# Two-part fp16 attention features with stacked heads, and neighbour counts from an extra mask column, in a four-layer graph kernel

## What is computed

```python
# layer 0: graph attention, 4 heads of 16
feats   = einsum('bnf,hfo->bhno', x, kernel)
f_self  = einsum('bnf,hfd->hbnd', x, attention_kernel)
f_other = einsum('bnf,hfd->hbdn', x, attention_kernel_2)
s = adj * einsum('hbnd,hbdm->hbnm', f_self, f_other)
s = where(s >= 0, s, 0.2 * s) / 4 + where(adj == 0, -1e9, 0)
attn = softmax(s, -1) * (adj != 0)
x = layernorm(x + relu(einsum('bhnm,bhmo->bhno', attn, feats) + bias))
# layer 1: A = adj + eye
x = layernorm(x + (A @ x) / sum(A, -1))
# layer 2
x = layernorm(x + adj @ (x @ weight) + bias2)
# layer 3
t = adj @ x
x = layernorm(x + where(t > 0.5, 1, 0))
```

## Time and profile before

| | us |
|---|---|
| median of 3 runs | 1572.43 |
| the 3 runs | 1569.07, 1574.97, 1572.43 |
| span of the profiled execution, first to last instruction | 1570.0 |
| median less that span | 2.4 |
| PE busy in the profile | 1379.7 (88%) |
| DVE busy | 1273.9 (81%) |
| ACT busy | 1235.0 (79%) |
| POOL busy | 1061.9 (68%) |

### The profile page before, as it was taken

One profiled execution on the slowest core, in us unless ns is written; L12 is line 12 of the kernel. 1 busy time (PEld: TensorE's weight loads), 2 busy tenths in 40 slices (PEclk: granted clock), 3 DMA queues, 4 the chain that ended last, 5 costly groups with the idle time before them and its releaser, 6 DMA issues.

```text
span 1570.0 us, 21762 instructions
## 1 busy us (share of the span) xinstructions
PE 1379.7 (88%) x7584; PEld 689.3 (44%) x7584; DVE 1273.9 (81%) x1518; ACT 1235.0 (79%) x1428; POOL 1061.9 (68%) x566
## 2 busy tenths in 40 slices
PE   4698799999899999999989988999899989799766
PEld 2343344454445444444444544454444444345323
DVE  1689789888898878888878888988889878878864
ACT  2598788887888878888878888888888888788631
POOL 3176866778677766787657876777767876776412
PEclk9899789999999989999979999999999999999977
DMA  7634433343433433343433434335333433200000
GB/s 107 111 42 81 47 73 67 56 54 58 88 43 77 47 65 62 58 71 38 83 62 54 57 52 95 45 64 61 51 75 62 69 38 73 58 14 16 26 11 10
DMA packets 144980, 91.16 MB, mean 58 GB/s; under 512 B 102420, under 2 KB 132570, under 8 KB 144858
## 3 DMA queue, kind: packets, MB, share of 16 engines
q1 hardware_dynamic: 129382, 70.44, 21.0%
q0 software_dynamic: 14288, 18.70, 14.8%
q10 hardware_dynamic: 1200, 0.63, 0.2%
HBM read 103.33 MB, written 21.38 MB: 79 GB/s over the span
## 4 chain that ended last, share of the span: by engine, by line
PE 50%; DVE 15%; issue 13%; ACT 9%; POOL 9%; DMA 2%; SPq 1%; ACTq 0%; DVEq 0%; POOLq 0%
PE M L607 10%; PE Z L568 10%; PE M L662 9%; PE Z L570 8%; POOL LS L501 7%; DVE RP L904 5%; ACT LS L754 5%; PE Z L581 4%; DVE LS L918 4%; PE Z L676 3%; PE Z L616 2%; ACT LS L762 2%; DMA adj_cast<-in_adj_dram 1%; PE Z L730 1%; DVE X L1000 1%
## 5 line engine op out<-in xcount | busy, mean ns | idle before, releaser
L501 POOL TENSOR_TENSOR LS<-LS,MB 125x1000 f32<-125x1000 f32 x372 | 871.1, 2359 | 360.7 <-DVE LS L918 264.8
L754 ACT ACTIVATE LS<-Z 125x1000 f32<-125x1000 f32 x576 | 576.3, 1002 | 143.5 <-PE Z L570 142.6
L762 ACT ACTIVATE LS<-LS 125x1000 f32<-125x1000 f32 x576 | 596.7, 1037 | 70.5 <-POOL LS L501 53.8
L904 DVE TENSOR_TENSOR RP<-LS,RP 125x1000 f32<-125x1000 f32 x480 | 575.4, 1199 | 88.3 <-ACT LS L754 66.3
L568 PE MATMUL Z<-AT,BI 126*125 126x500 fp8e4 x1152 | 375.9, 409 | 104.7 <-ACT LS L754 73.9
L570 PE MATMUL Z<-FS,FO 96*125 96x500 bf16 x1152 | 353.1, 388 | 0.0
L607 PE MATMUL M<-LS,V 125*18 125x500 f32 x2304 | 318.3, 626 | 5.5 <-ACT LS L762 5.5
L918 DVE TENSOR_TENSOR LS<-LS,MB 125x1000 f32<-125x1000 f32 x204 | 306.1, 1505 | 7.7 <-DMA MB<-row_maxima 2.4
L568 PEld LDWEIGHTS Z<-AT,BI 126*125 126x125 bf16 x1152 | 126.7, 142 | 418.2 <-ACT LS L754 219.2
L570 PEld LDWEIGHTS Z<-FS,FO 96*125 96x125 bf16 x1152 | 164.5, 143 | 95.0 <-issue 14.8
L662 PE MATMUL M<-AT,XP 125*128 125x500 fp8e4 x756 | 192.3, 377 | 0.0
(11 more groups left out here) (136 smaller groups left out, 885.0 us busy)
## 6 DMA issues: line engine op xcount, KB each, us to landing
MB<-row_maxima SPq DMA_DIRECT2D x48, 500.0 KB, 4.0
adj_cast<-in_adj_dram POOLq DMA_DIRECT2D x96, 183.1 KB, 4.4
FO<-PARTS SPq DMA_DIRECT2D x180, 46.9 KB, 2.1
FS<-PARTS SPq DMA_DIRECT2D x180, 46.9 KB, 2.1
XP<-in_x_dram SPq DMA_DIRECT2D x8, 336.0 KB
XA<-in_x_dram SPq DMA_DIRECT2D x8, 336.0 KB
out_dram<-X SPq DMA_DIRECT2D x7, 375.0 KB
AT<-adj_cast SPq DMA_TRANSPOSE x144, 2.8
```

Of the source, the lines that this page charges most:

```text
L501: nc.gpsimd.tensor_tensor(rows, rows, MB[:P, u % 2, :, :], ALU.subtract).then_inc(sub_pool, 1)
L754: nc.scalar.activation(LS[:P, q % RL, :, :], banks("Z", q)[:P], ACT.Prelu, alpha=SLOPE).then_inc(bent, 1)
L762: nc.scalar.activation(rows, rows, ACT.Exp, scale=0.25).then_inc(exps, 1)
L904: nc.vector.tensor_tensor(run, rows, run, ALU.max).then_inc(maxed, 1)
```

## The change

1. **Two fp16 parts.** `TERMS` has four pairs of two parts instead of six pairs of three. ACT's `middle` and DVE's `rest` are gone; `low` takes the difference straight from PSUM to the second part. `SPARE`, `MIDDLES`, `LOWS` and two semaphores are gone.
2. **Heads stacked.** `FS` holds the 2 x 64 rows of a pair of heads. `FO` keeps one plane for each head, with zeros in the 64 rows of the other, so a score matmul runs over 128 rows instead of 96. `FO` is set to zero once, at the start.
3. **Neighbour counts.** `BI` gets a 126th column of ones, so the mask matmul writes the sums of a tile's columns to row 125 of `Z`. ACT bends 126 rows, and `V` gets a 126th row that is one in the 18th column of the even heads and zero elsewhere. `weigh` contracts over 126 rows and so collects the counts. `degrees` and `DS` are gone, and `weigh` starts its sums in every unit.
4. **Rows in an own buffer.** `XF` no longer shares memory; its load waits for "XT" of the graph before, and `square` no longer waits for "XT".
5. `LS` has 26 slots instead of 24. `GROUP` = 1 and `CUTS` = 3 write the old order in another way.

```diff
+PD = P + 1
-TERMS = [(0, 0), (0, 1), (0, 2), (1, 0), (1, 1), (2, 0)]
+TERMS = [(0, 0), (0, 1), (1, 0), (1, 1)]
...
-RL = 24
+RL = 26
...
-MIDDLES = {19: 0, 26: 1, 31: 2}
-LOWS = {18: 0, 27: 1, 32: 2}
...
-        FS = sb("FS", [KS, H, N], bf16)
-        FO = sb("FO", [KS, H, N], bf16)
+        FS = sb("FS", [2 * KS, PAIRS, N], f16)
+        FO = sb("FO", [2 * KS, H, N], f16)
-        V = sb("V", [P, 2, NT, H, VC], f32)
+        V = sb("V", [PD, 2, NT, H, VC], f32)
-        PARTS = sb("PARTS", [128, 3, N], bf16)
+        PARTS = sb("PARTS", [128, 2, N], f16)
-        XF = SQ
+        XF = sb("XF", [P, NT, F], f32)
-        BI = sb("BI", [P + 1, P], bf16)
+        BI = sb("BI", [PD, PD], bf16)
...
             def load_parts(dst, sem_, side, h):
                 for n, pair in enumerate(TERMS):
-                    sp.dma_start(dst[n * D:(n + 1) * D],
+                    first = h % 2 * KS + n * D
+                    sp.dma_start(dst[first:first + D],
                                  PARTS[side * F + h * D:side * F + (h + 1) * D, pair[side], :]).then_inc(sem_, 16)
...
                 load_parts(FO[:, h, :], fo_in[p], 1, h)
-                load_parts(FS[:, h, :], fs_in[p], 0, h)
+                load_parts(FS[:, p, :], fs_in[p], 0, h)
...
-                        sp.wait_ge(dve_seq, link_of(b - 2, 3, 2))
+                    if b:
+                        sp.wait_ge(m1_filled, counted["XT", b, NS - 1] + 1)
+                    else:
+                        sp.wait_ge(pre_x, NS)
                     load_rows(b + 1, XF, xf_in)
...
-                    nc.tensor.matmul(z[:P, hh, :], BI[:, :], AT[:P + 1, g % RS, pair, PAD:CP, k], start=True, stop=False)
+                    nc.tensor.matmul(z[:PD, hh, :], BI[:, :], AT[:P + 1, g % RS, pair, PAD:CP, k], start=True, stop=False)
...
                     last = nc.tensor.matmul(z[:P, hh, :], FO[:, 2 * p + hh, m * P:(m + 1) * P],
-                                            FS[:, 2 * p + hh, s * C:(s + 1) * C], start=False, stop=True)
+                                            FS[:, p, s * C:(s + 1) * C], start=False, stop=True)
...
-            def degrees(u):
...
-                    last = nc.tensor.matmul(M0[VW * n:VW * n + VC, 0:C], V[:, b % 2, e % STEPS, 2 * p + hh, :], LS[:P, e % RL, hh, :],
-                                            start=(p == 1 and j == 0), stop=(j == STEPS // 2 - 1), skip_group_check=True)
+                    last = nc.tensor.matmul(M0[VW * n:VW * n + VC, 0:C], V[:, b % 2, e % STEPS, 2 * p + hh, :], LS[:PD, e % RL, hh, :],
+                                            start=(j == 0), stop=(j == STEPS // 2 - 1), skip_group_check=True)
...
-                nc.scalar.activation(LS[:P, q % RL, :, :], banks("Z", q)[:P], ACT.Prelu, alpha=SLOPE).then_inc(bent, 1)
+                nc.scalar.activation(LS[:PD, q % RL, :, :], banks("Z", q)[:PD], ACT.Prelu, alpha=SLOPE).then_inc(bent, 1)
...
-                nc.scalar.activation(PARTS[:, 1, c * C:(c + 1) * C], rest, ACT.Copy).then_inc(mid_ready, 1)
...
-                if l == 0 and b + 2 < B:
-
-                    act.wait_ge(m1_filled, counted["XT", b + 2, NS - 1] + 1)
                 nc.scalar.activation(SQ, Y[:, :, :], ACT.Square).then_inc(squared, 1)
...
+            nc.vector.memset(FO[:, :, :].rearrange("k h n -> k (h n)").bitcast(f32), 0.0)
+            nc.vector.memset(V[96:PD, :, :, :, 0:D + 1], 0.0).then_inc(v_set, 1)
+            nc.vector.memset(V[:, :, :, 0:H:2, D + 1:D + 2], 1.0).then_inc(v_set, 1)
+            nc.vector.memset(V[:, :, :, 1:H:2, D + 1:D + 2], 0.0).then_inc(v_set, 1)
...
-            def rest(b, c, bank, rest_):
...
-                nc.vector.tensor_tensor(PARTS[:, 2, c * C:(c + 1) * C], rest_, PARTS[:, 1, c * C:(c + 1) * C],
+                nc.vector.tensor_tensor(PARTS[:, 1, c * C:(c + 1) * C], bank[:, 0:C], PARTS[:, 0, c * C:(c + 1) * C],
                                         ALU.subtract).then_inc(lo_ready, 1)
```

More of the change, by code:

```diff
@@ L35 @@
 TURN = 3
+GROUP = 1
 LAG = 18
@@ L261, in y_at @@
         def y_at(q):
-            for n in range(3 * NS):
+            for n in range(CUTS * NS):
                 at = layer_at(q, Y0 + n)
                 if at and at[1] < 3:
-                    return (*at, *divmod(n, 3))
+                    return (*at, *divmod(n, CUTS))
             return None
@@ L286, in adj_resnorm @@
         for q in range(END):
-            if q < QN:
-                ring.append(("Z", q))
+            if q < QN and q % GROUP == 0:
+                for n in range(GROUP):
+                    ring.append(("Z", q + n))
             if w_at(q):
@@ L549, in ring_free, with masks @@
                     pe.wait_ge(added, 9 * b + 3 * l + c + 1)
-            def fill_z(q):
+            def masks(q):
                 u, m = divmod(q, STEPS)
@@ L582, in turn_run @@
                 last.then_inc(run_turned, 1)
-            def degrees(u):
-                b, i = divmod(u, UPG)
-                g = NS * b + i
-                pe.wait_ge(o4_ready, u + 1)
-                for n in range(NS):
-                    for k in range(ST):
-                        nc.tensor.matmul(M0[VW * k:VW * k + VC, 0:C], DS[:, :], AT[:P, g % RS, KK * n + k // KK, PAD:CP, k % KK],
-                                         start=(n == 0), stop=False, skip_group_check=True)
             def weigh(w):
@@ L660, in collect @@
                     pe.wait_ge(xp_ready, 3 * b + l + 1)
-                for m in range(ST * part, ST * (part + 1)):
+                for m in range(NT // CUTS * part, NT // CUTS * (part + 1)):
                     last = nc.tensor.matmul(M1[:, 0:C], XP[:, m, :], AT[:P, (NS * b + c) % RS, m // KK, PAD:CP, m % KK],
                                             start=(m == 0), stop=(m == NT - 1 and l > 0))
-                if part == 2 and l == 0:
+                if part == CUTS - 1 and l == 0:
                     last = own_rows(M1, c)
-                if part == 2:
+                if part == CUTS - 1:
                     last.then_inc(m1_filled, 1)
@@ L701, in _ @@
             for q in range(END):
-                if q < QN:
-                    fill_z(q)
+                if q < QN and q % GROUP == 0:
+                    for n in range(GROUP):
+                        masks(q + n)
+                    for n in range(GROUP):
+                        scores(q + n)
                 if feature_at(q):
@@ L707, in _ @@
                     collect(*y_at(q))
-                if unit_at(q, DEGREE_AT) is not None and unit_at(q, DEGREE_AT) % UPG < NS:
-                    degrees(unit_at(q, DEGREE_AT))
                 if w_at(q):
@@ L835, in _ @@
                 for n, pair in enumerate(TERMS):
-                    act.dma_start(FS[n * D:(n + 1) * D, h, :], PARTS[h * D:(h + 1) * D, pair[0], :]).then_inc(fs_in[0], 16)
+                    first = h * KS + n * D
+                    act.dma_start(FS[first:first + D, 0, :], PARTS[h * D:(h + 1) * D, pair[0], :]).then_inc(fs_in[0], 16)
             act.wait_ge(ones_in, 1)
@@ L849, in _ @@
                     square(*layer_at(q, SQUARE))
-                if r in MIDDLES and b + 1 < B:
-                    middle(b + 1, MIDDLES[r], REST[:, :])
-                if q < QN:
-                    bend(q)
+                if q < QN and q % GROUP == 0:
+                    for n in range(GROUP):
+                        bend(q + n)
                 at = layer_at(q, HIGH)
```

61 lines of the change are left out of this document (27 added, 34 removed).

## The result

The changed kernel takes 1550.29 us (median of 4 runs, 1540.79 to 1557.14), against 1573.7 for the kernel before on the same chip: a ratio of 0.9863, with a 95% interval of 0.9816 to 0.9909. The recorded ratios come from the single runs and are not exactly the quotient of the two medians, which is 0.985 here. A second set on another chip (e11) gave 0.9881 (0.9851 to 0.9910); a seventh execution of that set took 2461.22 us, 1.6 times as long as the six others, and is left out of it. So the change makes the kernel faster by 1.2 to 1.4%, some 19 to 23 us, where I had forecast 39.5 us. The profiled execution is the slowest of the four: 1557.14 us, a span of 1555.3 and a mean granted clock of 0.931. The four clocks were 0.931, 0.940, 0.939 and 0.945 for 1557.14, 1546.63, 1553.94 and 1540.79 us.

A forecast was written before the change was run, and what follows sets the result against it. No engine was full: ACT set a floor of 1.81 us a step, with further ACT work, PE-bound stretches and stalls above. Terms 14.4 + 5.2 + 6.0 + 7.1 + 1.4 + 5.4 = 39.5 us gave 1533 us, range 1512 to 1560.

The forecast's parts named there:

- rival A: After r=20, PE becomes the new wait at r=23; 18.4 us less gain, 1551 us; chance 0.20.
- the queue's: Sign of right: row_maxima issued within 0.3 us of the reduction's end, MB 2.2 us later, no ACT idling at r=20.
- B: Rival: PE loses up to 17.8 us of work, new slow-clock stretches cost 5.45 us each, say 1609 us; chance 0.17.
- Fewer DMAs of parts: SP's queue: 8 instead of 12 DMAs per head remove ACT's stalls at r=20 in graphs 2 to 7; 14.4 us.
- D: Rival: the store still blocks the maxima in SP's queue; 5.5 us less gain, 1538 us; chance 0.55 together with the forecast.
- Graph 0: ACT's waits at r=17 and 20 go, 5.2 us; its wait for maxima behind r=39 and 41 goes, 6.0 us.
- Fewer parts to make: ACT loses its middle copies; those at r=19 and 31 in seven graphs win 0.51 us each, 7.1 us.
- My bound of 0: Lower bound of the 7.1 us for ACT's removed copies, if PE or POOL is next.
- The clock of graph 4: The half-speed stretch at r=22 to 27 after the 2.25 us stall goes; 5.4 us, bounds 0 and twice that.
- Start, own buffer, score matmul: Kernel-start memsets, separate row buffer and 128-row fp16 score matmuls: no gain or cost; uncovered memsets would cost 4.5 us once.
- The counts: Removing PE's bursts of 12 matmuls wins 0.2 us at r=35 in seven graphs, 1.4 us; upper bound 17.8 us.

The follow-up runs named there:

- e11: The changed kernel itself, unaltered, run again on another chip, against the kernel before: ratio 0.9881.
- e3: The changed kernel with four further DMAs per head into a tile nothing reads (12 again) and 24 slots of LS: 1580.17 us, ratio 1.0051.
- e7: The changed kernel with POOL's low part of the layer input one step later (LOW 6 instead of 5): 1545.46 us, ratio 0.9887.
- e4: The changed kernel with POOL's four adjacency loads moved from r=27, 29, 31, 33 to r=36, 38, 40, 42: 1551.40 us, ratio 0.9863.
- e2: The kernel before without its bursts of 12 matmuls, neighbour counts left out: 1578.35 us, ratio 1.0033.
- e9: The changed kernel with bursts of 12 matmuls that nothing reads, at r=35, 47 and 11: 1520.96 us, ratio 0.9709.
- e1: The changed kernel with bursts of 12 matmuls that nothing reads put back at r=23, 35 and 47: 1538.21 us, ratio 0.9770.
- e12: e1 unaltered, run again on another chip, against the kernel before: 1537.48 us, ratio 0.9808.

## Why the prediction was partly right

The measured 1550 us lies in the range of 1512 to 1560, and 17 us above the forecast of 1533. It lies next to the 1551 of rival A, but A's main step, a new wait at r = 23 to 26, did not happen. The range reached so far up because of A; that it also covered the loss of clock at r = 35 and 47 is in part luck. Of the signs that I had named, the queue's came true as right, and the clock of 0.931 with long steps in new places came true as wrong (B).

- **Fewer DMAs of parts (14.4 us): right, mechanism and size.** ACT's stalls at r = 20 of graphs 2 to 7 are gone, and these steps are 13.9 us shorter; the maxima left 0.03 us after they were ready, and `MB` followed in 2.08 us (2.2 forecast). e3 shows that the DMA count does this. Rivals A and D fall: no wait appears at r = 23 to 26, and the store is out of the way at 768.12.
- **Graph 0 (5.2 and 6.0 us).** The second came as 6.5. The first came as 3.9 (r = 16, 17 and 20): `row_maxima` was issued at 64.52 and `MB` only at 68.43, 3.9 us later and not 2.2, so ACT still waits 1.42 and 0.81 us for POOL.
- **Fewer parts to make (7.1 us): half.** r = 18 and r = 30 are 0.5 us shorter in seven graphs each, and r = 26 gave nothing on balance, as said. But what r = 30 gave, r = 33 took back with interest. The failed step is "in stretches where ACT sets the pace": it did at r = 31, but not two steps on: summed over r = 30 to 33, graphs 1 to 6 are 0.1 to 0.4 us longer than before. Next was POOL, whose low part waits for ACT's high part (shown by e7, after e4 had ruled out the loads) and whose subtraction behind it takes 0.4 us more than before. My bound of 0 for "PE or POOL is next" was the right one for this half.
- **The clock of graph 4 (5.4 us): right.** 19.22 us became 13.78. This was no chance of one execution: in e2, which keeps the old queue, the same steps of graph 4 take 18.71 us at a clock of 0.58, and in e3, where the stalls are back, graphs 2 to 6 take 15.2 to 16.3 us at 0.73 to 0.78.
- **Start, own buffer, score matmul (0): no cost shows.** The first `bend` starts at 36.75 us, before at 36.77. A pair of score matmuls takes 0.59 us at full clock in both kernels, with 96 rows of bf16 and with 128 of fp16. e9 takes r = 46 to 50 in the same 7.98 us as the kernel before.
- **The counts (1.4 us): wrong, in sign and size.** The failed step is "Below nothing the term cannot go by the burst itself", with the clock left out of the term. The row at r = 47 was read rightly: the burst lay in PE's wait and its own time was worth nothing. What I did not ask is what PE does in that wait once the burst is gone. At r = 47 it idles 1.33 us instead of 0.59, and the clock falls in all eight graphs; at r = 35 it idles 1.41 to 1.62 us instead of 0.67 at most, and the clock falls in five. That cost 21.2 us at these two places in the profiled execution, which was the slowest of the four, and 11 to 12 us in the medians (e1, e12). Even the 0.2 us at r = 35 were not the burst's: r = 34 to 38 take 9.74 us in graph 4 both with it (e1) and without.
- **Rival B** had this mechanism ("PE loses up to 17.8 us of work") with a wrong price. I took 5.45 us for a new slow stretch, from one six-step stretch in graph 4. The new ones cost 0.8 to 2.5 us each, and hold for 2 to 4 steps. I also set B against my forecast, one or the other. In truth both happened at once: with the bursts put back the change wins 30 to 34 us (1567.94 - 1537.48 in e12, 1572.04 - 1538.21 in e1), and B takes a third of that.

In the sum: against 39.5 us forecast stand 30 to 34 us with the clock loss taken out. The 6 to 9 us between are the copy at r = 31, the 1.3 us in graph 0 and the counts, and what is left is within the spread of the executions. The 11 to 12 us that are missing beyond that are the clock. Four kernels on one chip show the two effects side by side: the kernel before 1572.04, without bursts 1578.35 (e2); the change with bursts 1538.21 (e1), and e3, the change with neither bursts nor the shorter queue, 1580.17. Leaving out the bursts costs 6 us with the old queue and 11 to 12 with the new one.
